# A Sobel stage: its contraction in three chunks of 128 rows in place of four of 96, the bias as a float32r product, and its loops written out

## The chip, the cores and the metric

The kernel runs on one core of one Trainium2 chip. The metric is the device time of one execution in microseconds (us). The kernel is one program of seven stages that follow one another; the change touches one of them, which takes some 290 us of the 3580.

## What is computed

Four image blocks follow one another on x (2 images, 192 channels, 112 by 112, f32): window attention with an MLP, a Sobel block, a ConvNeXt block, and a merged depthwise convolution. The Sobel block is the one that matters here:

```python
edge_x = _depthwise3x3(x, sobel_x, c)
edge_y = _depthwise3x3(x, sobel_y, c)
edges = jnp.concatenate([edge_x, edge_y], axis=1)          # 384 channels
fused = jnp.einsum('bchw,oc->bohw', edges, fusion_w) + fusion_b[None, :, None, None]
mu = jnp.mean(fused, axis=1, keepdims=True)
var = jnp.mean(jnp.square(fused - mu), axis=1, keepdims=True)
normed = (fused - mu) * jax.lax.rsqrt(var + EPS)
normed = normed * ln_w[None, :, None, None] + ln_b[None, :, None, None]
return x + jax.nn.gelu(normed, approximate=False)
```

## The kernel before

The MLP stage ahead of this one has already made the horizontal halves of both Sobel filters and stored them in DRAM: `d["u"]` (differences, for edge_x) and `d["v"]` (smoothed, for edge_y). The function `sobel` works through 28 steps (`NS`, 14 strips of 8 lines in each of 2 images). A strip is 7 blocks (`BX`) of 128 pixels. In words, step t goes through the engines so:

- **SP** loads four tiles, u and v for each half k of the channels (`xu`, `xv`, 96 partitions each, one buffer for each). Each load waits until VectorE has used up the tile of the step before. It stores the finished strip of five steps before (`SLAG`) from `X` to `scratch_x2`.
- **DVE** (VectorE) makes the vertical halves in `edges(t, k)`: an add of two views of `xu` (L1119) and a subtraction of two views of `xv` (L1122) into `edge`, which has two buffers. So L1119 waits until PE is done with step t-2 (`fused`). Between `edges(t, 0)` and `edges(t, 1)` stand the end of step t-4, `X + f` (L1131), which waits for the gelu, and the scale and shift of the normalised step t-3 (L1136 by `ln_w`, then L1138 by `ln_b`, which waits for L1136).
- **PE** (TensorE) makes, for each of the 7 blocks, one product of 384 rows in four chunks of 96 (L1187). The bias is a 97th row in the first chunk: a row of ones in `edge`, the bias in `wf`. The columns of the weights and of the bias are centred beforehand, so the mean of the result is zero. Each f32 product is two instructions for PE, so a step has 56. PSUM holds two steps; PE waits until the step two before has been read (`normed`).
- **ACT** (ScalarE) takes in its body for step t, in this order: the gelu of step t-4 (L1160), two squares with a sum of step t-1 (L1152), the seven scaled copies of step t-2 out of PSUM (L1168, `normed`; they wait for the reciprocal deviation `rs` and for L1131 of step t-4, which frees the buffer of `f`), and the other five squares of step t-1.
- **POOL** (GpSimd) adds epsilon to the seven sums (L1092, reads one small tile) and raises them to the power -0.5 (L1096, reads two) for step t-2.

The loops of all five queues run over two steps at a time (`run_steps` with U = 2) behind a head of 6 steps written out; SP loops over one step at a time. Nothing else orders the work: each engine takes its instructions in the order in which they are written, and waits on semaphores.

Of the kernel before, what the change touches and what calls it, by code (L numbers as in the profile page):

```python
# [14 lines left out]
ALU = mybir.AluOpType  # L15
# [994 lines left out]
def sobel(nc, a, d, X, PS, stack):  # L1010

    s = Scope(nc, "sobel", stack)

    wf = s.sb("wf", [CH + 1, 2 * KC, C])
    mean = s.sb("mean", [CH + 1, 2 * KC])
# [10 lines left out]
    uloaded, vloaded = s.sems("uloaded", KC), s.sems("vloaded", KC)  # L1026
    q = {x: s.sem(x) for x in ("wloaded", "ready", "wsum", "wmean", "centred", "ex", "ey", "fused", "squared", "var_ok",
                               "rstd", "normed", "scaled", "affine", "gelu", "added", "stored")}
    U, HEAD, LAG = 2, 6, 4
    SLAG = 5  # L1030
    READY = 2

    def psF(t, j):
        return PS[:, 4 * t.buf(2) + j // 2, j % 2 * 256:j % 2 * 256 + C]

    def in_blocks(t, e):
        return view(edge[0:CH, t.buf(2), e, 0, 0:1], [[8, 8], [64, 2 * BX], [1, 8]])

    def per_block(i):
        return view(row[:, i, 0:1], [[0, BX], [1, C]])  # L1040
# [1 line left out]
    def rows8(ap):  # L1042
        return ap.rearrange("p r (b c) -> p r b c", c=8)

    with nc.Block() as block:
        @block.sync
        def _(sp):
            sp.dma_start(wf[0:CH, :, :], a["L1_conv_fusion_wT"].rearrange("(k p) n -> p k n", p=CH)).then_inc(q["wloaded"], 16)
            sp.dma_start(wf[CH:CH + 1, 0, :], a["L1_conv_fusion_b"].partition_broadcast(1)).then_inc(q["wloaded"], 16)
# [16 lines left out]
            for img in range(IMG):  # L1066
                for j in range(SLAG):
                    t = Step(0, img * BY + j, 1)
                    load(t, img, 8 * j)
                    if t.reached(SLAG):  # L1070
                        store(t.back(SLAG))
                with sp.Fori(SLAG, BY) as g:
                    load(Step(g, img * BY, 1), img, g * 8)
                    store(Step(g, img * BY - SLAG, 1))
            for j in range(NS - SLAG, NS):
                store(Step(0, j, 1))
            sp.wait_ge(q["stored"], 16 * NS)

        @block.gpsimd
        def _(pool):  # L1080
            nc.gpsimd.memset(edge[CH:CH + 1, :, 0, :, :], 1.0).then_inc(q["ready"], 1)
            pool.wait_ge(q["ready"], 1)
            nc.gpsimd.memset(mhalf[:, :], -0.5).then_inc(q["ready"], 1)
            pool.wait_ge(q["ready"], 2)
# [12 lines left out]
            run_steps(pool, NS, U, HEAD, LAG, body)  # L1097

        @block.vector
        def _(dve):  # L1100
            dve.wait_ge(q["wloaded"], 64)
            for e in range(2 * KC):
                rows = CH + 1 if e == 0 else CH
                nc.vector.reduce_sum(mean[0:rows, e:e + 1], wf[0:rows, e, :], AX.X).then_inc(q["wsum"], 1)
            dve.wait_ge(q["wsum"], 2 * KC)
            for e in range(2 * KC):
                rows = CH + 1 if e == 0 else CH
                nc.vector.tensor_scalar(mean[0:rows, e:e + 1], mean[0:rows, e:e + 1], 1.0 / C, None, ALU.mult).then_inc(q["wmean"], 1)
            dve.wait_ge(q["wmean"], 2 * KC)
            for e in range(2 * KC):  # L1110
                rows = CH + 1 if e == 0 else CH
                nc.vector.tensor_scalar(wf[0:rows, e, :], wf[0:rows, e, :], mean[0:rows, e:e + 1], None, ALU.subtract).then_inc(q["centred"], 1)

            def edges(t, k):
                dve.wait_ge(uloaded[k], t.n * 16 + 16)
                if t.reached(2):
                    dve.wait_ge(q["fused"], t.n * BX - BX)
                u = xu[:, k, :, :]
                nc.vector.tensor_tensor(in_blocks(t, k), rows8(u[:, 0:8, :]), rows8(u[:, 1:9, :]), ALU.add).then_inc(q["ex"], 1)  # L1119
                dve.wait_ge(vloaded[k], t.n * 16 + 16)  # L1120
                v = xv[:, k, :, :]
                nc.vector.tensor_tensor(in_blocks(t, KC + k), rows8(v[:, 2:10, :]), rows8(v[:, 0:8, :]), ALU.subtract).then_inc(q["ey"], 1)  # L1122

            def body(t):
                if t.inside(NS):
                    edges(t, 0)
                c = t.back(4)
                if c.inside(NS):
                    dve.wait_ge(q["gelu"], c.n + 1)
                    strip = X[:, bass.ds(c.n * BX, BX), :]  # L1130
                    nc.vector.tensor_tensor(strip, strip, f[:, c.buf(2), :, :], ALU.add).then_inc(q["added"], 1)  # L1131
                b = t.back(3)
                if b.inside(NS):
                    fb = f[:, b.buf(2), :, :]
                    dve.wait_ge(q["normed"], b.n * BX + BX)
                    nc.vector.tensor_tensor(fb, fb, per_block(0), ALU.mult).then_inc(q["scaled"], 1)  # L1136
                    dve.wait_ge(q["scaled"], b.n + 1)
                    nc.vector.tensor_tensor(fb, fb, per_block(1), ALU.add).then_inc(q["affine"], 1)  # L1138
                if t.inside(NS):
                    edges(t, 1)  # L1140
            run_steps(dve, NS, U, HEAD, LAG, body)

        @block.scalar
        def _(act):
# [10 lines left out]
            def body(t):  # L1155
# [15 lines left out]
            run_steps(act, NS, U, HEAD, LAG, body)  # L1171

        @block.tensor
        def _(pe):
            pe.wait_ge(q["wloaded"], 64)
            pe.wait_ge(q["ready"], READY)
            pe.wait_ge(q["centred"], 2 * KC)

            def body(t):
                pe.wait_ge(q["ex"], t.n * KC + KC)  # L1180
                pe.wait_ge(q["ey"], t.n * KC + KC)
                if t.reached(2):
                    pe.wait_ge(q["normed"], t.n * BX - BX)
                for j in range(BX):
                    for e in range(2 * KC):
                        rows = CH + 1 if e == 0 else CH
# [441 lines left out]
```

## Time and profile before

| what | value |
|---|---|
| time, median of 3 runs | 3580.73 us (3580.53 to 3581.01) |
| the profiled execution's own time | 3581.64 us |
| its span | 3579.5 us |
| sobel stage: first load to first load of the next stage | 1825.9 to 2120.2 us |
| PE in it: first to last product | 1839.6 to 2101 us |

The profiled execution is 0.9 us slower than the median, and 2.1 us of it lie outside the span. Columns of the timeline are start, duration, engine, line, operation, output and inputs with their shapes; in brackets is the idle time of the engine ahead of the row and what ended it. Spans of POOL are rough. PE's mean durations (326 ns) are latencies; the pace is read from the distance between starts.

### The profile page before, as it was taken

The numbers are of one execution on the slowest core, as the hardware profiler recorded it, in microseconds if no ns is written. First come the engines' busy times: TensorE is split into PE (matmuls) and PEld (weight loads), VectorE is DVE, ScalarE is ACT, GpSimd is POOL, SyncE is SP. The second block draws the span as 40 slices with busy tenths as digits, with TensorE's granted clock in tenths as the row PEclk, the third lists the DMA queues.
The fourth block names the chain that finished last, engine by engine and source line by source line (L and its number), as shares of the span: only waits on it lengthen the run. The fifth ranks groups of instructions, "written<-read, shape, count | busy, mean of one in ns | idle before, by whom it ended". The sixth has DMA issues, their size and how long they took to land. (4 is left out here: it accounts for less than half of the span.)

```text
span 3579.5 us, 95798 instructions
## 1 busy us (share of the span) xinstructions
PE 3423.4 (96%) x31958; PEld 3312.3 (93%) x31958; DVE 2389.3 (67%) x5936; ACT 1790.2 (50%) x5312; POOL 1080.1 (30%) x1951
## 2 busy tenths in 40 slices
PE   7999999999799999999969969989999899989999
PEld 6888888888699999999969969989999899989999
DVE  5777777777556666666659979979999311125554
ACT  4666666666444444444426657659999200002222
POOL 3233333333244444444425520014444223320000
PEclk9999999999899999999989989999999899999999
DMA  1455566610011111111158865537777788877775
GB/s 34 123 197 192 198 239 235 233 58 23 23 34 51 51 51 51 50 51 51 50 141 256 247 188 198 196 124 201 198 198 199 221 253 253 251 228 228 227 227 174
DMA packets 472671, 554.97 MB, mean 155 GB/s; under 512 B 78259, under 2 KB 331957, under 8 KB 472373
## 3 DMA queue, kind: packets, MB, share of 16 engines
q1 hardware_dynamic: 447028, 531.65, 49.3%
q10 hardware_dynamic: 25344, 19.27, 1.7%
q8 instruction: 196, 3.21, 0.4%
q14 instruction: 103, 0.84, 0.1%
HBM read 392.56 MB, written 271.52 MB: 186 GB/s over the span
## 5 line engine op out<-in xcount | busy, mean ns | idle before, releaser
L1325 PE MATMUL PS<-dw_grid,dw_mats 128*128 128x196 f32 (+1 forms) x3840 | 624.0, 326 | 37.0 <-DVE dw_mats L1266 37.0
L1325 PEld LDWEIGHTS PS<-dw_grid,dw_mats 128*128 128x128 f32 x3840 | 623.5, 191 | 37.5 <-DVE dw_grid L1262 37.5
L1297 ACT ACTIVATE dw_res<-PS,dw_brow 128x196 f32<-128x196 f32 x192 | 81.5, 424 | 699.3 <-PE PS L1325 699.3
L981 PE MATMUL PS<-mlp_w,mlp_hid 128*128 128x192 f32 x2352 | 414.0, 326 | 0.5 <-ACT mlp_hid L796 0.5
L1262 DVE COPY dw_grid<-X 32x392 f32 (+3 forms) x480 | 290.3, 605 | 171.8 <-PE PS L1325 148.7
L1560 PE MATMUL PS<-gain,down_hid 128*128 128x192 f32 x2352 | 385.4, 328 | 3.6 <-DMA down_hid<-scratch_hid 3.6
L1560 PEld LDWEIGHTS PS<-gain,down_hid 128*128 128x128 f32 x2352 | 385.1, 191 | 3.9 <-DMA down_hid<-scratch_hid 3.9
L981 PEld LDWEIGHTS PS<-mlp_w,mlp_hid 128*128 128x128 f32 x2352 | 378.3, 190 | 0.8 <-ACT mlp_hid L796 0.8
L796 ACT ACTIVATE mlp_hid<-PS,mlp_b 128x256 f32<-128x256 f32 x588 | 247.0, 471 | 110.8 <-PE PS L787 110.8
L1187 PE MATMUL PS<-sobel_wf,sobel_edge 96*128 96x192 f32 (+1 forms) x1568 | 261.0, 328 | 29.2 <-DVE sobel_edge L1122 28.9
L1187 PEld LDWEIGHTS PS<-sobel_wf,sobel_edge 96*128 96x128 f32 (+1 forms) x1568 | 257.3, 191 | 32.9 <-issue 32.8
L1548 DVE TENSOR_TENSOR X<-PS,down_x 128x192 f32 (+1 forms) x196 | 70.0, 357 | 319.2 <-PE PS L1560 317.6
L796 ACT ACTIVATE hid_hid<-PS,hid_b 128x256 f32<-128x256 f32 x588 | 237.0, 471 | 34.4 <-PE PS L787 34.4
L529 ACT ACTIVATE att_vbd<-PS 64x96 f32<-64x96 f32 x784 | 194.4, 248 | 109.4 <-PE PS L625 102.5
L854 POOL COPY X<-mlp_x 128x192 f32 (+1 forms) x196 | 113.5, 579 | 429.0 <-DVE mlp_x L926 427.8
L537 ACT ACTIVATE att_qk<-PS,att_qbias 128x256 f32<-128x256 f32 x392 | 164.7, 471 | 148.6 <-PE PS L652 148.6
L926 DVE TENSOR_TENSOR mlp_x<-PS,X 128x192 f32<-128x192 f32 x196 | 70.0, 357 | 212.8 <-PE PS L981 195.2
L408 POOL TENSOR_SCALAR att_xn<-att_x,att_mv,att_rs 128x192 f32<-128x192 f32 x196 | 198.5, 1022 | 20.1 <-POOL att_rs L401 20.1
L397 POOL TENSOR_SCALAR att_ve<-att_mv 128x2 f32<-128x2 f32 x98 | 22.6, 231 | 593.9 <-DVE att_mv L440 593.9
L1540 POOL TENSOR_TENSOR down_x<-down_x,cvec 128x192 f32<-128x192 f32 x196 | 115.7, 590 | 272.1 <-DMA down_x<-scratch_x 272.1
L473 DVE TENSOR_REDUCE att_mx<-PS 128x8 f32<-128x512 f32 x196 | 135.6, 692 | 71.3 <-PE PS L641 71.2
L787 PE MATMUL PS<-mlp_ha_hi,mlp_wa_hi 128*128 128x256 f32 x588 | 174.7, 297 | 0.0
(217 smaller groups left out, 9284.2 us busy)
## 6 DMA issues: line engine op xcount, KB each, us to landing
scratch_hid<-hid_hid SPq DMA_DIRECT2D x196, 384.0 KB, 3.7
down_hid<-scratch_hid SPq DMA_DIRECT2D x196, 384.0 KB, 4.0
scratch_wide<-scratch_taps SPq DMA_DIRECT2D x64, 960.0 KB, 5.3
dw_raw<-scratch_wide SPq DMA_DIRECT2D x96, 640.0 KB, 4.3
scratch_wide<-scratch_taps SPq DMA_DIRECT2D x64, 768.0 KB, 4.7
dw_raw<-scratch_wide SPq DMA_DIRECT2D x96, 512.0 KB, 3.3
sobel_xv<-scratch_v SPq DMA_DIRECT2D x56, 420.0 KB, 5.0
scratch_u<-mlp_u SPq DMA_DIRECT2D x56, 378.0 KB, 3.0
```

The lines of the kernel that those rows point to most:

```text
L408: nc.gpsimd.tensor_scalar(xn[:, i, :], x[:, t.buf(XR) - 1 + i, :], mv[:, t.buf(4) - 1 + i, 0:1], rs[:, i:i + 1], ALU.subtract, ALU.mult).t ...
L473: nc.vector.reduce_max(mx[:, b.buf(2), :].rearrange("p (h e) -> p h e", e=2), s4, AX.X).then_inc(q["max"], 1)
L529: last = nc.scalar.activation(vbd[64 * e:64 * e + 64, b.buf(4), w, :, e, 0:HD], src, ACT.Identity)
L537: nc.scalar.activation(qk[:, u.buf(2), ch, :], psQK[i], ACT.Identity, bias=qbias[:, ch:ch + 1]).then_inc(q["qk_ready"], 1)
L787: last = nc.tensor.matmul(self.psU[i][:, e * 256:(e + 1) * 256], w[:, m], h, start=(j == 0), stop=(j == len(terms) - 1))
L796: last = nc.scalar.activation(hid[:, m, :], self.psU[i][:, e * 256:(e + 1) * 256], ACT.Gelu, bias=self.b1[:, m:m + 1])
L981: last = nc.tensor.matmul(psD[i], hid[:, p.buf(2), m, i * 128:(i + 1) * 128], w2[:, m, :], start=(m == 0), stop=(m == MC - 1))
L1187: last = nc.tensor.matmul(psF(t, j), edge[0:rows, t.buf(2), e, j, :], wf[0:rows, e, :], start=(e == 0), stop=(e == 2 * KC - 1))
L1262: last = nc.vector.tensor_copy(dst, src)
L1325: last = nc.tensor.matmul(dst[:, :, ys, :], m, src, start=(i == 0), stop=(i == len(steps) - 1))
L1540: nc.gpsimd.tensor_tensor(x2[:, b.buf(R), :], x2[:, b.buf(R), :], cvec[:, :], ALU.add).then_inc(q["resid"], 1)
L1560: last = nc.tensor.matmul(PS[:, b.buf(R), 0:C], hid[:, b.buf(R), m, :], gain2[:, img, m, :], start=(m == 0), stop=(m == MC - 1))
```

## The change

The 384 rows of the contraction are cut at 128 and 256 in place of 96, 192 and 288. The rows are 192 of u and 192 of v, so the middle chunk holds the last 64 of u and the first 64 of v, both in a tile `xm` of 128 partitions. There are still four edge operations for VectorE in a step (`OPS`): u on 128 partitions, u on 64, v on 64, v on 128, all with the 896 elements in a partition that there were before. In a body for step t the two of u now stand ahead of the work for t-4 and t-3, and the two of v behind it. `xu` and `xm` have two buffers each, `xv` one.

The 97th row has no room in a full chunk. The bias becomes a fourth product for each block, `ones_r` by `bias_r`, over 33 rows in float32r: row 0 holds the bias rounded to float32r, row 32 what the rounding left, and the rows between are zero. VectorE makes these rows ahead of the first step, which takes three more operations (L1112, L1122, L1125). The two DMAs that bring the bias wait for GpSimd's clearing of the tile and are issued behind the four loads of step 0. All loops of the stage are written out (`unrolled`).

```diff
-    wf = s.sb("wf", [CH + 1, 2 * KC, C])
+    wf = s.sb("wf", [128, KT, C])
+    bias_r = s.sb("bias_r", [PARTS, C], F32R)
+    ones_r = s.sb("ones_r", [PARTS, 128], F32R)
-    xu = s.sb("xu", [CH, KC, 9, HW])
-    xv = s.sb("xv", [CH, KC, 10, HW])
-    edge = s.sb("edge", [CH + 1, 2, 2 * KC, BX, 128])
+    xu = s.sb("xu", [128, 2, 9, HW])
+    xm = s.sb("xm", [128, 2, 10, HW])
+    xv = s.sb("xv", [128, 1, 10, HW])
+    edge = s.sb("edge", [128, 2, KT, BX, 128])
...
+            def load(t):
...
+                parts = ((xu, slice(0, 128), 9, u[0:128]), (xm, slice(0, REST), 9, u[128:C]),
+                         (xm, slice(REST, 128), 10, v[0:REST]), (xv, slice(0, 128), 10, v[REST:C]))
+                for i, (ring, rows, lines, src) in enumerate(parts):
+                    n = ring.shape[1]
+                    if t.reached(n):
+                        sp.wait_ge(q["edges"], (t.n - n) * OPS + i + 1)
+                    sp.dma_start(ring[rows, t.buf(n), 0:lines, :], src).then_inc(loaded[i][t.buf(n)], 16)
...
+            load(Step(0, 0, NS))
+            sp.wait_ge(q["ready"], 1)
+            for at_ in (0, PARTS - 1):
+                sp.dma_start(bias[at_:at_ + 1, :], a["L1_conv_fusion_b"].partition_broadcast(1)).then_inc(q["wloaded"], 16)
...
             def body(t):
                 if t.inside(NS):
-                    edges(t, 0)
+                    across(t, 0, 0, slice(0, 128), xu)
+                    across(t, 1, 1, slice(0, REST), xm)
...
                 if t.inside(NS):
-                    edges(t, 1)
-            run_steps(dve, NS, U, HEAD, LAG, body)
+                    along(t, 2, 1, slice(REST, 128), xm)
+                    along(t, 3, 2, slice(0, 128), xv)
+            unrolled(NS, 4, body)
...
                 for j in range(BX):
-                    for e in range(2 * KC):
-                        rows = CH + 1 if e == 0 else CH
-                        last = nc.tensor.matmul(psF(t, j), edge[0:rows, t.buf(2), e, j, :], wf[0:rows, e, :], start=(e == 0), stop=(e == 2 * KC - 1))
+                    nc.tensor.matmul(psF(t, j), ones_r[:, :], bias_r[:, :], start=True, stop=False)
+                    for k in range(KT):
+                        last = nc.tensor.matmul(psF(t, j), edge[:, t.buf(2), k, j, :], wf[:, k, :], start=False, stop=(k == KT - 1))
                     last.then_inc(q["fused"], 1)
-            run_steps(pe, NS, U, HEAD, 0, body)
+            unrolled(NS, 0, body)
```

On VectorE, one step of the loop before, from its first edge operation on; REGISTER_ALU and ISA rows are address and semaphore work of the loop:

```order
L1119 TENSOR_TENSOR sobel_edge<-sobel_xu 96x8x14x8
L1122 TENSOR_TENSOR sobel_edge<-sobel_xv 96x8x14x8
L1129 REGISTER_ALU
L1131 ISA
L1131 TENSOR_TENSOR X<-X,sobel_f 128x1344
L1135 ISA
L1136 TENSOR_TENSOR sobel_f<-sobel_f,sobel_row 128x1344
L1137 REGISTER_ALU
L1138 TENSOR_TENSOR sobel_f<-sobel_f,sobel_row 128x1344
```

One step of the change at the same place (steady state):

```order
L1133 TENSOR_TENSOR sobel_edge<-sobel_xu 128x8x14x8
L1133 TENSOR_TENSOR sobel_edge<-sobel_xm 64x8x14x8
L1149 TENSOR_TENSOR X<-X,sobel_f 128x1344
L1154 TENSOR_TENSOR sobel_f<-sobel_f,sobel_row 128x1344
L1156 TENSOR_TENSOR sobel_f<-sobel_f,sobel_row 128x1344
L1139 TENSOR_TENSOR sobel_edge<-sobel_xm 64x8x14x8
L1139 TENSOR_TENSOR sobel_edge<-sobel_xv 128x8x14x8
```

There are still seven operations in a step and the same three in the middle; two u operations stand ahead of them in place of a u and a v, and the rows of the loop's own work are gone.

On SP's queue at the start of the stage, before:

```order
L1048 DMA sobel_wf<-in_L_conv_fusion_wT 96x4x192
L1049 DMA sobel_wf<-in_L_conv_fusion_b 1x192
L1051 DMA sobel_row<-in_L_conv_ln_w 128x192
L1051 DMA sobel_row<-in_L_conv_ln_b 128x192
L1057 DMA sobel_xu<-scratch_u 96x1008
L1060 DMA sobel_xv<-scratch_v 96x1120
L1057 DMA sobel_xu<-scratch_u 96x1008
L1060 DMA sobel_xv<-scratch_v 96x1120
```

and now:

```order
L1054 DMA sobel_wf<-in_L_conv_fusion_wT 128x3x192
L1056 DMA sobel_row<-in_L_conv_ln_w 128x192
L1056 DMA sobel_row<-in_L_conv_ln_b 128x192
L1067 DMA sobel_xu<-scratch_u 128x1008
L1067 DMA sobel_xm<-scratch_u 64x1008
L1067 DMA sobel_xm<-scratch_v 64x1120
L1067 DMA sobel_xv<-scratch_v 128x1120
L1076 DMA sobel_bias<-in_L_conv_fusion_b 1x192 x2
L1067 DMA sobel_xu<-scratch_u 128x1008
L1067 DMA sobel_xm<-scratch_u 64x1008
```

The bias was second; it is now two transfers behind the loads of step 0, and the loads of step 1 follow without a wait but for `xv`.

On PE, the loop before:

```order
L99 UNCONDITIONAL_BRANCH
L99 ISA
L1183 ISA
L1187 MATMUL PS<-sobel_wf,sobel_edge 128x192 x28
L1180 ISA
L1183 ISA
L1187 MATMUL PS<-sobel_wf,sobel_edge 128x192 x28
```

and the first blocks of the change, written out:

```order
L1201 MATMUL PS<-sobel_bias_r,sobel_ones_r 128x192
L1203 MATMUL PS<-sobel_wf,sobel_edge 128x192 x3
L1201 MATMUL PS<-sobel_bias_r,sobel_ones_r 128x192
L1203 MATMUL PS<-sobel_wf,sobel_edge 128x192 x3
L1201 MATMUL PS<-sobel_bias_r,sobel_ones_r 128x192
```

A block was four products of one kind; it is now one float32r product and three f32 products.

## Rows read from the trace of the kernel before

**Rows 1.** Stretch 1900 to 1950: busy us (instructions) of PE, PEld, DVE, ACT, POOL; clock, DMA share, GB/s.

```profile
1900.00:1950.00 50.00, 49.91 (x303) 49.04 (x302) 47.17 (x39) 30.28 (x115) 27.05 (x11) 1.00 0.87 258
```

**Rows 2.** Waits, 1860 to 2100: engine, line, releaser: total us, times, longest.

```profile
ACT sobel_f L1168 <- POOL sobel_rs L1096: 54.2, 24, 3.2
...
DVE sobel_edge L1119 <- PE PS L1187: 18.7, 24, 5.4
...
PEld PS L1187 <- issue: 3.7, 12, 0.4
```

**Rows 3.** Timeline of ACT, 1851 and 1860: start us, us; the waits in brackets.

```profile
1851.25 0.33 ACT L1152 ACTIVATE sobel_sq<-PS 128x192 bf16<-128x192 f32 x1 [0.57 <-PE PS L1187]
...
1860.37 0.33 ACT L1152 ACTIVATE sobel_sq<-PS 128x192 bf16<-128x192 f32 x1 [0.57 <-PE PS L1187]
```

**Rows 4.** Timeline of DVE, 1906 to 1926, two steps and a piece.

```profile
1906.33 1.09 DVE L1119 TENSOR_TENSOR sobel_edge<-sobel_xu 96x896 f32<-96x896 f32 x1 [0.24 <-PE PS L1187]
...
1907.34 1.08 DVE L1122 TENSOR_TENSOR sobel_edge<-sobel_xv 96x896 f32<-96x896 f32 x1
...
1908.34 1.55 DVE L1131 TENSOR_TENSOR X<-X,sobel_f 128x1344 f32 x1
...
1911.40 1.56 DVE L1138 TENSOR_TENSOR sobel_f<-sobel_f,sobel_row 128x1344 f32<-128x1344 f32 x1
...
1913.87 1.08 DVE L1122 TENSOR_TENSOR sobel_edge<-sobel_xv 96x896 f32<-96x896 f32 x1
...
1917.97 1.56 DVE L1131 TENSOR_TENSOR X<-X,sobel_f 128x1344 f32 x1
...
1926.88 1.55 DVE L1131 TENSOR_TENSOR X<-X,sobel_f 128x1344 f32 x1
```

**Rows 5.** Timeline of POOL, 1906 to 1921.

```profile
1906.99 0.54 POOL L1092 TENSOR_SCALAR sobel_ve<-sobel_ss 128x7 f32<-128x7 f32 x1 [4.60 <-ACT sobel_sq L1152]
...
1907.70 5.03 POOL L1096 TENSOR_TENSOR sobel_rs<-sobel_ve,sobel_mhalf 128x7 f32<-128x7 f32 x1 [0.16 <-POOL sobel_ve L1092]
...
1918.11 2.79 POOL L1096 TENSOR_TENSOR sobel_rs<-sobel_ve,sobel_mhalf 128x7 f32<-128x7 f32 x1 [0.16 <-POOL sobel_ve L1092]
```

**Rows 6.** Timeline of ACT, 1912 to 1918.

```profile
1912.77 2.29 ACT L1168 ACTIVATE sobel_f<-PS,sobel_rs 128x192 f32<-128x192 f32 x7 [2.65 <-POOL sobel_rs L1096]
...
1916.42 1.41 ACT L1160 ACTIVATE sobel_f<-sobel_f 128x1344 f32<-128x1344 f32 x1
```

**Rows 7.** Timeline of PE at 700 (float32r terms) and at 1507 (plain f32).

```profile
700.66 0.34 PE L625 MATMUL PS<-att_wa_hi,att_ha_hi 128*128 128x192 f32 x1
700.83 0.28 PE L625 MATMUL PS<-att_wa_lo,att_ha_hi 128*128 128x192 f32 x1
700.94 0.27 PE L625 MATMUL PS<-att_wa_hi,att_ha_lo 128*128 128x192 f32 x1
...
1507.17 2.11 PE L981 MATMUL PS<-mlp_w,mlp_hid 128*128 128x192 f32 x12
...
1509.12 0.60 PE L758 MATMUL PS<-mlp_ident,mlp_xn 128*128 128x128 f32 x4
```

**Rows 8.** Timeline of all engines at the start of the sobel stage.

```profile
1827.11 0.41 SPq L1051 DMA_DIRECT2D sobel_row<-in_L_conv_ln_b  x1
...
1832.92 1.13 DVE L1104 TENSOR_REDUCE sobel_mean<-sobel_wf 97x1 f32<-97x192 f32 x4 [10.72 <-DMA sobel_row<-in_L_conv_ln_b]
...
1835.37 1.08 DVE L1119 TENSOR_TENSOR sobel_edge<-sobel_xu 96x896 f32<-96x896 f32 x1
...
1839.60 2.90 PE L1187 MATMUL PS<-sobel_wf,sobel_edge 97*128 97x192 f32 x8 [28.85 <-DVE sobel_edge L1122]
```

**Rows 9.** Stretch 1835 to 1837, columns as in rows 1.

```profile
1835.00:1837.00 2.00, 0.00 (x0) 0.00 (x0) 2.00 (x4) 0.00 (x0) 0.00 (x0) 0.50 0.65 160
```

**Rows 10.** Timeline of POOL, then of DVE, at 1852.

```profile
1852.61 2.18 POOL L1096 TENSOR_TENSOR sobel_rs<-sobel_ve,sobel_mhalf 128x7 f32<-128x7 f32 x1
...
1853.33 1.08 DVE L1119 TENSOR_TENSOR sobel_edge<-sobel_xu 96x896 f32<-96x896 f32 x1
```

More of the change, by code:

```diff
@@ L1025, in sobel, with in_blocks @@
     mhalf = s.sb("mhalf", [128, BX])
-    uloaded, vloaded = s.sems("uloaded", KC), s.sems("vloaded", KC)
-    q = {x: s.sem(x) for x in ("wloaded", "ready", "wsum", "wmean", "centred", "ex", "ey", "fused", "squared", "var_ok",
+    loaded = [s.sems("loaded%d_" % i, 2) for i in range(4)]
+    q = {x: s.sem(x) for x in ("wloaded", "ready", "wsum", "wmean", "centred", "edges", "fused", "squared", "var_ok",
                                "rstd", "normed", "scaled", "affine", "gelu", "added", "stored")}
-    U, HEAD, LAG = 2, 6, 4
     SLAG = 5
-    READY = 2
+    READY = 3
+    OPS = 4
     def psF(t, j):
         return PS[:, 4 * t.buf(2) + j // 2, j % 2 * 256:j % 2 * 256 + C]
-    def in_blocks(t, e):
-        return view(edge[0:CH, t.buf(2), e, 0, 0:1], [[8, 8], [64, 2 * BX], [1, 8]])
+    def in_blocks(t, e, rows):
+        return view(edge[rows, t.buf(2), e, 0, 0:1], [[8, 8], [64, 2 * BX], [1, 8]])
     def per_block(i):
@@ L1064, in store @@
                 sp.dma_start(d["x2"][bass.ds(t.n * BX, BX)].rearrange("b p c -> p b c"), X[:, bass.ds(t.n * BX, BX), :]).then_inc(q["stored"], 16)
[L1066 to L1074, printed above, removed]
+            load(Step(0, 0, NS))
+            sp.wait_ge(q["ready"], 1)
+            for at_ in (0, PARTS - 1):
+                sp.dma_start(bias[at_:at_ + 1, :], a["L1_conv_fusion_b"].partition_broadcast(1)).then_inc(q["wloaded"], 16)
+            for j in range(1, NS):
+                load(Step(0, j, NS))
+                if j >= SLAG:
+                    store(Step(0, j - SLAG, NS))
             for j in range(NS - SLAG, NS):
-                store(Step(0, j, 1))
+                store(Step(0, j, NS))
             sp.wait_ge(q["stored"], 16 * NS)
@@ L1080, in _ @@
         def _(pool):
-            nc.gpsimd.memset(edge[CH:CH + 1, :, 0, :, :], 1.0).then_inc(q["ready"], 1)
+            nc.gpsimd.memset(bias[:, :], 0.0).then_inc(q["ready"], 1)
             pool.wait_ge(q["ready"], 1)
+            nc.gpsimd.memset(ones[:, :], 1.0).then_inc(q["ready"], 1)
             nc.gpsimd.memset(mhalf[:, :], -0.5).then_inc(q["ready"], 1)
-            pool.wait_ge(q["ready"], 2)
+            pool.wait_ge(q["ready"], READY)
             def body(t):
@@ L1106, in _ @@
[L1106 to L1115, printed above, removed]
+            rows = [wf[:, k, :] for k in range(KT)] + [bias[:, :]]
@@ new lines, in _ @@
+            means = [mean[:, k:k + 1] for k in range(KT)] + [mean[0:PARTS, KT:KT + 1]]
+            dve.wait_ge(q["wloaded"], 16 * 5)
+            dve.wait_ge(q["ready"], READY)
+            nc.vector.tensor_copy(ones_r[:, :], ones[:, :])
+            for r, m in zip(rows, means):
+                nc.vector.reduce_sum(m, r, AX.X).then_inc(q["wsum"], 1)
+            dve.wait_ge(q["wsum"], KT + 1)
+            for m in means:
+                nc.vector.tensor_scalar(m, m, 1.0 / C, None, ALU.mult).then_inc(q["wmean"], 1)
@@ new lines, in _ @@
+            dve.wait_ge(q["wmean"], KT + 1)
+            for r, m in zip(rows, means):
+                nc.vector.tensor_scalar(r, r, m, None, ALU.subtract).then_inc(q["centred"], 1)
+            dve.wait_ge(q["centred"], KT + 1)
+            nc.vector.tensor_copy(bias_r[:, :], bias[:, :]).then_inc(q["centred"], 1)
+            dve.wait_ge(q["centred"], KT + 2)
+            low = slice(PARTS - 1, PARTS)
+            nc.vector.tensor_tensor(bias_r[low, :], bias[low, :], as_f32(bias_r[low, :]), ALU.subtract).then_inc(q["centred"], 1)
@@ L1121, in edges, with along @@
-                v = xv[:, k, :, :]
-                nc.vector.tensor_tensor(in_blocks(t, KC + k), rows8(v[:, 2:10, :]), rows8(v[:, 0:8, :]), ALU.subtract).then_inc(q["ey"], 1)
+                nc.vector.tensor_tensor(in_blocks(t, k, rows), rows8(src[:, 0:8, :]), rows8(src[:, 1:9, :]), ALU.add).then_inc(q["edges"], 1)
+            def along(t, i, k, rows, src):
+                n = src.shape[1]
+                src = src[rows, t.buf(n), :, :]
+                dve.wait_ge(loaded[i][t.buf(n)], t.turn(n) * 16 + 16)
+                nc.vector.tensor_tensor(in_blocks(t, k, rows), rows8(src[:, 2:10, :]), rows8(src[:, 0:8, :]), ALU.subtract).then_inc(q["edges"], 1)
@@ L1139, in body @@
                 if t.inside(NS):
[L1140 to L1141 removed]
+                    along(t, 2, 1, slice(REST, 128), xm)
+                    along(t, 3, 2, slice(0, 128), xv)
+            unrolled(NS, 4, body)
         @block.scalar
```

40 lines of the change are left out of this document (14 added, 26 removed).

## The prediction

> **What bounds the kernel now.** The stages follow one another, so I read only the stretch of this stage, by windows first. Between 1900 and 1950 us PE is busy for 49.91 of 50 us at the full clock, DVE for 47.17, ACT for 30.28, and the DMA engines for 0.87 of the time [rows 1]. So PE sets the pace, but DVE is 5% behind it, and that decides this case. The waits agree: PE waits for nobody; its weight loads meet 12 short gaps of issue, 3.7 us in all; DVE waits for PE (18.7 us in 24 times), ACT for POOL's L1096 (54.2 us) [rows 2].
>
> The pace, part by part. In the steps written out ahead of the loop the last block of a step reaches ACT at 1851.25 and of the next at 1860.37, with ACT waiting for PE both times: 9.12 us for a step [rows 3], which is 56 products of 0.163 us. In the loop two steps take 18.54 us (L1131 at 1908.34 and at 1926.88) [rows 4], or 9.27 for one; the 0.30 above twice 9.12 are what one turn of the loop costs PE.
>
> DVE's own step, read from start to start where it has no idle time: L1119 at 1906.33, L1131 at 1908.34, L1138 at 1911.40, the last L1122 at 1913.87, and 1.01 more for it (the distance of the first two rows): 8.55 us [rows 4].
>
> Then a round through four engines. L1131 starts at 1908.34. POOL has begun L1096 at 1907.70, but it takes 5.03 us and ends at 1912.73, that is 1.33 behind the start of L1138 at 1911.40 [rows 4, 5]. L1138 waits for L1136, so there DVE is free for an instant. ACT's L1168 starts at 1912.77 and takes 2.29, then come five squares, the gelu at 1916.42 for 1.41, and the next L1131 at 1917.97 [rows 4, 6]. From L1131 to L1131 that is 9.63 us without any wait for PE. In the next step L1096 begins at 1918.11, just behind the start of L1131 that had waited for the gelu, and takes 2.79 [rows 5]; that round is short. I call these the long and the short step; they alternate over the whole loop. The long one gets its length from POOL being held off by DVE.
>
> **The change part by part.**
>
> PE. Removed: 2 of 8 f32 instructions in each block, so 6 stay. Plain f32 products of 192 columns go at 1.95 us for 12 (L981 at 1507.17 to L758 at 1509.12), 0.1625 each [rows 7]. Added: a float32r product of 192 columns. The same width stands in the attention: 0.17 us from the first of a run to the second, 0.11 from the second to the third [rows 7]. In the change every one stands between f32 products, so I take the 0.17; bounds 0.11 and, if it went like f32, 0.33. A block becomes 6 x 0.1625 + 0.17 = 1.145, a step 8.0 us against 9.12 (bounds 7.6 and 9.1). PE alone would give 28 x (9.27 - 8.0) = 35 us.
>
> DVE. Four edge operations of 896 elements in a partition stay four, whatever the partitions; I cost them unchanged, and the step at 8.55. So from the step on in which all seven operations are there, DVE covers most of PE's gain.
>
> Where the stall goes. With PE at 8.0 it no longer fills the time; the long step of 9.63 is made of DVE, POOL and ACT alone and is untouched by the change. What follows depends on how often it comes:
> - It alternates as now: 9.63 and then 8.55 (DVE without idle), 9.09 for a step.
> - It never comes: 8.55.
> - I take one long in three: (9.63 + 8.55 + 8.55) / 3 = 8.91. PE starts its product when L1168 has freed PSUM, 6.7 us behind the long step's L1131 (1915.06 against 1908.34 [rows 4, 6]), and ends it 8.0 later, which is 5.1 behind the next L1131. So the sums reach POOL while the last edge operation of DVE's step runs, and L1096 falls between the two u operations. The one L1096 that began with only edge operations around it began at 1852.61 and took 2.18, so it got in at the next boundary, 1853.33 [rows 10]. A step later PE's end falls some 1 us later against DVE, L1096 begins right ahead of L1131 as at 1907.70, and is held for long again.
>
> Sum for the steps: the first three steps have no L1131 yet, and behind the last product comes a tail that no edge operation holds up, so four steps gain PE's full 9.12 - 8.0 = 1.12, 4.5 us. The other 24 gain 9.27 - 8.91 = 0.36, 8.6 us. The loop's 0.30 a turn is inside that.
>
> The start of the stage costs. Today ln_b, issued at 1827.11, lands at 1832.92; DVE takes 2.45 us for the centring and 4.2 for the edges, and PE starts at 1839.60 [rows 8]. In the change the last thing that DVE waits for is the bias, behind four loads of 1.6 MB in the same queue. The DMA engines are still at 0.65 between 1835 and 1837 [rows 9], where step 0's loads end, so I take 1837 for its landing: 4 us later. The three added small operations, each with a semaphore, take some 1 us (a group of four reductions took 1.13 in the same place [rows 8]). Together 5 us; bounds 1 (the small transfers slip past) and 8 (they land with a wait of their own). What is queued behind that wait is all of DVE, and PE behind it; nothing hides it.
>
> Nothing for the rest: POOL's clearing of one row is replaced by two short ones, 10 us ahead of their use; ACT has 20 of 50 us idle [rows 1]. The second buffers I cost at nothing: DVE does not wait for a load among its waits now. But the loads stand in SP's order behind `xv`, which is single and waits for the end of DVE's step, so u and the middle of the next step have one DVE step, as now. DMA work is 0.87 x 9.27 = 8.1 us a step [rows 1], under 8.55, so the cover holds at 8.91 with 0.8 to spare and at 8.55 with 0.5.
>
> Sum: 5.0 - 4.5 - 8.6 = -8.1 us, -0.23%. The profiled execution stands 0.9 above the median; taken from the median, 3580.7 - 8.1 = 3572.6 us.
>
> **The rivals.**
>
> - The round alternates as now, 9.09: for it speaks that it does so eleven times in the loop. 5.0 - 4.5 - 24 x 0.18 = -3.8: 3576.9 us.
> - POOL is never held for long, DVE fills its time, 8.55: -16.8 or, with the setup's lower bound, -20: 3563.9 us. For it speaks the short step, in which L1096 waits for one operation only [rows 5]. Against it the long step: begun at 1907.70, L1096 lets the ends of two operations pass and gets in at the third [rows 4, 5]. The Trainium skill, SBUF — State Buffer, section "A bandwidth-pool intuition that's wrong", has the blocked engine go on some 115 ns behind the end of the DVE operation; by that the long step would not exist, L1096 would end within 3 us of L1131, and the time would be this rival's. The trace disagrees in the long step.
> - Slower: the held time grows. If DVE has no idle time and also L1092 must wait for the instant ahead of L1138, L1096 begins 3.3 us behind L1131 and gets in only at the end of DVE's step at 6.6; 1.4 for itself, 2.3 for L1168 and 2.9 for squares and gelu make 13.2 in place of 9.63. Each such step costs 3.6 us; two cancel the forecast's gain, four or five make it slower than now by 0.2%, one in three gives 29 - 8 = +21: 3602 us. For it speaks that in the change DVE is nearly full; against it that L1092 now gets in at once (0.54 us at 1906.99, while an edge operation runs) [rows 5].
> - The float32r product costs as much as an f32 one: PE stays at 9.1, only the loop's 0.15 a step is won, and the setup costs: 5 - 4 = +1: 3582 us. The rows of the attention speak against it.
>
> **How the numbers follow.** A measurement tells 0.2%, 7.2 us, from no change. Chances: one long step in three or near it 0.36, half of it beyond 7.2; alternating 0.27, nearly all within; DVE filled 0.24; POOL starved 0.09; float32r dear or the start worse 0.04. That gives faster 0.47, same 0.43, slower 0.10. The range reaches from DVE filled with a cheap start (3561) to alternating with a dear start (3581). The forecast's own, with its start between 1 and 8 us, is 3568.6 to 3575.6.
>
> **What the profile of the change would show.** PE with idle time of 0.5 to 1 us ahead of each step, ended by the last edge operation or by ACT's copies out of PSUM, and a step's products over in 8.0 us. A mean distance of the additions to X of 8.9; rows of the -0.5 power of 5 us in one step of three. PE's first product 5 us later behind the stage's first load, with DVE waiting for the bias. DVE's share above 0.95. The forecast is wrong if the power's rows are all short (then 3564), all or half long (3577 or more), or if DVE waits for loads.

## The result, and the profile after

The changed kernel takes 3612.88 us (median of 4 runs, 3605.15 to 3613.77), the kernel before 3580.87 (3580.53 to 3581.72): a ratio of 1.0082, 95% interval 1.0067 to 1.0097. It is slower by 0.8%, where 0.2% faster was forecast, and outside the range.

The same stretch as [rows 1], of the changed kernel (busy us of PE, PEld, DVE, ACT, POOL; clock, DMA share, GB/s):

```profile
1900.00:1950.00 50.00, 50.00 (x243) 39.03 (x243) 43.18 (x35) 28.62 (x107) 29.00 (x10) 1.00 0.81 233
```

PE is still the busy one, at the full clock, with 243 instructions in place of 303. DVE has lost 4 us of work. So PE does fewer instructions and each takes longer. The weight loads (PEld) had filled 49.04 us; now 11 of 50 are free. The waits of the stretch of [rows 2] say where:

```profile
ACT sobel_f L1187 <- POOL sobel_rs L1103: 61.4, 22, 2.9
DVE sobel_edge L1133 <- PE PS L1203: 44.1, 24, 7.8
...
PEld PS L1201 <- issue: 37.3, 166, 0.2
```

DVE waits for PE in every step, and the engine's weight-load side stands idle 166 times ahead of the bias product's weights, with nothing named as the releaser ("issue"). One and a half blocks on PE, weight loads first, then matmuls:

```profile
1911.06 0.18 PEld L1201 LDWEIGHTS PS<-sobel_bias_r,sobel_ones_r 33*128 33x128 f32 x1 [0.23 <-issue]
1911.34 0.95 PEld L1203 LDWEIGHTS PS<-sobel_wf,sobel_edge 128*128 128x128 f32 x6
1912.51 0.18 PEld L1201 LDWEIGHTS PS<-sobel_bias_r,sobel_ones_r 33*128 33x128 f32 x1 [0.22 <-issue]
...
1911.06 0.35 PE L1201 MATMUL PS<-sobel_bias_r,sobel_ones_r 33*128 33x192 f32 x1
1911.34 1.24 PE L1203 MATMUL PS<-sobel_wf,sobel_edge 128*128 128x192 f32 x6
1912.51 0.35 PE L1201 MATMUL PS<-sobel_bias_r,sobel_ones_r 33*128 33x192 f32 x1
```

From one L1201 to the next is 1.45 us: 0.28 to the first f32 product, and 1.17 for six instructions that at 0.1625 each should take 0.975. The weight load of L1201 begins when its matmul begins, not ahead of it, and that of the next L1203 too. Neither switch, into the bias product or out of it, has its weights ready. A step of seven such blocks takes 10.17 us, against 9.27 before:

```profile
1901.06 1.09 DVE L1133 TENSOR_TENSOR sobel_edge<-sobel_xu 128x896 f32<-128x896 f32 x1 [1.32 <-PE PS L1203]
...
1907.71 1.09 DVE L1139 TENSOR_TENSOR sobel_edge<-sobel_xm 64x896 f32<-64x896 f32 x1
1908.83 1.09 DVE L1139 TENSOR_TENSOR sobel_edge<-sobel_xv 128x896 f32<-128x896 f32 x1
1911.24 1.09 DVE L1133 TENSOR_TENSOR sobel_edge<-sobel_xu 128x896 f32<-128x896 f32 x1 [1.32 <-PE PS L1203]
```

The start, to be held against [rows 8]: the stage's first transfer, DVE's first instruction, PE's first product.

```profile
1828.87 0.42 SPq L1054 DMA_DIRECT2D sobel_wf<-in_L_conv_fusion_wT  x1
...
1839.88 0.22 DVE L1112 CAST sobel_ones_r<-sobel_ones 33x128 fp32r<-33x128 f32 x1 [14.76 <-DMA sobel_bias<-in_L_conv_fusion_b]
...
1847.70 0.50 PE L1201 MATMUL PS<-sobel_bias_r,sobel_ones_r 33*128 33x192 f32 x1 [34.04 <-DVE sobel_edge L1139]
```

PE starts 18.8 us behind the stage's first transfer (before: 13.7, from 1825.93 to 1839.60), so +5.2. The account: 28 x (10.17 - 9.27) = 25.2 and 5.2 give 30.4; from the stage's first transfer to that of the next stage it is 325.3 us against 294.3, +31.0. The spans differ by 32.5, the rest lying outside the stage. The stage itself starts 3 us later, but stage starts differ by that much between kernels that are alike up to there (1825.2 to 1831.9 in the runs below), so I compare lengths of the stage.

### The profile page after: what moved, and what is told of

It is laid out like the page before. It is cut to its first block and busy times, and to the rows that moved or that the text cites. A ratio compares the mean times of both kernels' runs of the same rounds, so it can differ in the third digit from the quotient of the medians.

```text
span 3612.0 us, 94747 instructions
## 1 busy us (share of the span) xinstructions
PE 3449.7 (96%) x31762; PEld 3278.8 (91%) x31762; DVE 2392.7 (66%) x5939; ACT 1787.8 (49%) x5312; POOL 1101.8 (31%) x1952
## 5 line engine op out<-in xcount | busy, mean ns | idle before, releaser
L796 ACT ACTIVATE hid_hid<-PS,hid_b 128x256 f32<-128x256 f32 x588 | 236.6, 470 | 34.3 <-PE PS L787 34.3
L1203 PE MATMUL PS<-sobel_wf,sobel_edge 128*128 128x192 f32 x1176 | 245.6, 346 | 0.0
L1203 PEld LDWEIGHTS PS<-sobel_wf,sobel_edge 128*128 128x128 f32 x1176 | 187.4, 191 | 19.4 <-issue 0.3
```

What stands on the lines that cost most here:

```text
L796: last = nc.scalar.activation(hid[:, m, :], self.psU[i][:, e * 256:(e + 1) * 256], ACT.Gelu, bias=self.b1[:, m:m + 1])
L1203: last = nc.tensor.matmul(psF(t, j), edge[:, t.buf(2), k, j, :], wf[:, k, :], start=False, stop=(k == KT - 1))
```

## The experiments

The theory after the result was that the switch of type, float32 to float32r and back, stops the weights from being loaded ahead. The rival was the switch of contraction rows, 128 to 33 and back. Each run changes only the sobel function, and its ratio is taken against runs of the kernel before on the same chip (their medians lie between 3580.0 and 3582.2 us, and a single run beside the last gave 3584.1).

**Bias product in plain float32, 33 rows.** With the ones at 0.5, as both rows now hold the whole bias:

```
-  nc.tensor.matmul(psF(t, j), ones_r[:, :], bias_r[:, :], start=True, stop=False)
+  nc.tensor.matmul(psF(t, j), ones[:, :], bias[:, :], start=True, stop=False)
```

> The changed kernel with the bias product as plain float32 (two instructions over the same 33 rows, ones of 0.5 against the bias in both rows, so the sum is the same). Nothing else moves. In the changed kernel a block takes 1.453 us, of which six float32 instructions at the pace of before (0.1625 us) explain 0.975. Theory 'switch' (going from float32 to float32r and back costs, because no weights are loaded ahead across it): there is no switch left, eight instructions at 0.1625 make a block of 1.30 us, a step of 9.1 us where it now is 10.17, and a time of 3613 - 28 x 1.06 = 3583 us. Rival 'rows' (going from 128 contraction rows to 33 and back costs): the cost stays and one more instruction comes on top, a block of 1.6 us, a step of 11.3, 3645 us.

Measured: 3940.19 us, ratio 1.1002 (1.0984 to 1.1021). Both theories missed it. A block by PE's timeline, and then the stretch's row, with columns as in [rows 1]:

```profile
1901.77 1.00 PE L1201 MATMUL PS<-sobel_bias,sobel_ones 33*128 33x192 f32 x2
1902.71 2.29 PE L1203 MATMUL PS<-sobel_wf,sobel_edge 128*128 128x192 f32 x6
```

```profile
1900.00:1950.00 50.00, 50.00 (x128) 36.02 (x127) 17.53 (x14) 12.77 (x48) 11.60 (x4) 0.50 0.36 109
```

The granted clock is 0.50 (1.2 GHz) through the whole stage, though PE is never idle. A block takes 22.07 / 7 = 3.15 us; eight instructions at twice 0.1625 are 2.60, so 0.55 remain for switches, with no change of type left. The type theory is in trouble, as it allows for no such remainder; the clock is a second effect of its own, and the last two runs take it up.

**Bias product over 128 rows, float32r.** `bias`, `bias_r`, `ones` and `ones_r` are 128 rows deep, with zeros between:

```
-    bias_r = s.sb("bias_r", [PARTS, C], F32R)
+    bias_r = s.sb("bias_r", [128, C], F32R)
```

> The changed kernel with the float32r bias product over all 128 rows (ones and bias_r are 128 rows deep, zeros in 31 and the last 95 rows of bias_r). The type still changes twice a block, the number of rows no longer does. Theory 'switch': nothing changes, block 1.45 us, step 10.17, 3613 us. Rival 'rows': the product costs what the attention rows gave for one in a run, 0.11 to 0.17 us, block 1.09 to 1.14, PE's step under 8.0, the step then set by the round of DVE, POOL and ACT at about 8.9, and 3613 - 28 x 1.27 = 3577 us.

Measured: 3578.69 us, ratio 0.9994 (0.9984 to 1.0003). PE's timeline, weight loads first:

```profile
1869.19 0.19 PEld L1201 LDWEIGHTS PS<-sobel_bias_r,sobel_ones_r 128*128 128x128 f32 x1
1869.35 0.95 PEld L1203 LDWEIGHTS PS<-sobel_wf,sobel_edge 128*128 128x128 f32 x6
...
1869.22 0.38 PE L1201 MATMUL PS<-sobel_bias_r,sobel_ones_r 128*128 128x192 f32 x1
1869.44 1.16 PE L1203 MATMUL PS<-sobel_wf,sobel_edge 128*128 128x192 f32 x6
1870.30 0.38 PE L1201 MATMUL PS<-sobel_bias_r,sobel_ones_r 128*128 128x192 f32 x1
```

The block is 1.086 us, six at 0.1625 and 0.11. The weights are loaded ahead of their matmul again (by 0.03 and 0.09 us, from start to start), across the same two changes of type. The type theory falls; rows it is, at 1.453 - 1.086 = 0.367 us for the two switches of a block. But the step is 9.30 us in the mean, not 8.9, so that the time came close to the 3577 of "rows" is partly luck: more below.

**The 33-row product twice in a row.** The bias is added twice, so the result of the kernel differs.

```
   nc.tensor.matmul(psF(t, j), ones_r[:, :], bias_r[:, :], start=True, stop=False)
+  nc.tensor.matmul(psF(t, j), ones_r[:, :], bias_r[:, :], start=False, stop=False)
```

> The changed kernel with the float32r bias product issued twice in each block, one right behind the other (the bias is added twice). Theory 'switch': the second product is already in its type and costs only its own pace, 0.11 us by the attention rows, so block 1.56 us, step 10.9, and 3613 + 28 x 0.77 = 3634 us. Rival 'each product is dear' (0.48 us for one of 33 rows, whatever stands ahead of it): block 1.93, step 13.5, 3706 us.

Measured: 3890.36 us, ratio 1.0865 (1.0847 to 1.0883), again at a granted clock of 0.50 throughout, so its time tells neither number. Its rows do:

```profile
1921.27 0.28 PEld L1201 LDWEIGHTS PS<-sobel_bias_r,sobel_ones_r 33*128 33x128 f32 x1 [0.44 <-issue]
1921.43 0.33 PEld L1202 LDWEIGHTS PS<-sobel_bias_r,sobel_ones_r 33*128 33x128 f32 x1
1921.94 1.78 PEld L1204 LDWEIGHTS PS<-sobel_wf,sobel_edge 128*128 128x128 f32 x6 [0.17 <-issue]
```

Of the two 33-row products only the second has its weights loaded ahead (from 1921.43, for a matmul at 1921.60). The idle time stands at the two switches (0.44 and 0.17 us), not at each product.

**65 rows, and 64.** These fix where the switch begins: `PARTS` 65 or 64 in place of 33.

> The changed kernel with the float32r bias product over 65 rows in place of 33 (zeros in all rows but 0 and 32). The run with 128 rows gave a block of 1.086 us, the changed kernel's 33 rows 1.453, and the kernel before went from 97 rows to 96 in every block at no cost to be seen (eight instructions at 0.1625 us). Theory 'row mode' (TensorE is drained when the number of contraction rows goes across 64, and not by other changes of it): 65 rows cost nothing extra, block 1.09 us, and the time is that of the 128-row run, 3579 us. Rival 'any narrower product' (a product that leaves the last quarter or half of the rows unused holds up the next): block stays between 1.2 and 1.45, 3590 to 3613 us.

> The same with 64 rows, one row less. Theory 'row mode': the drain is back in full, block 1.45 us, a step of 10.17, 3613 us. Rival (the cost depends on how many rows are unused): between the 65-row and the 33-row block.

Measured: 3579.49 us with 65 rows, ratio 0.9996 (0.9986 to 1.0005), and 3611.28 with 64 (one run). PE's timeline, of 65 and then of 64 rows:

```profile
1882.92 0.39 PE L1201 MATMUL PS<-sobel_bias_r,sobel_ones_r 65*128 65x192 f32 x1
1883.15 1.16 PE L1203 MATMUL PS<-sobel_wf,sobel_edge 128*128 128x192 f32 x6
```

```profile
1900.99 0.35 PE L1201 MATMUL PS<-sobel_bias_r,sobel_ones_r 64*128 64x192 f32 x1
1901.27 1.24 PE L1203 MATMUL PS<-sobel_wf,sobel_edge 128*128 128x192 f32 x6
1902.44 0.35 PE L1201 MATMUL PS<-sobel_bias_r,sobel_ones_r 64*128 64x192 f32 x1
```

One row makes the whole difference: 64 rows give the block of 33 rows (1.45, step 10.17), 65 rows that of 128 (step 9.30). The Trainium skill, TensorEngine Tiling (Array Packing), section "Tiling Modes", has row tilings of 32, 64 and 128 rows and says that changing the mode drains the engine (the work in it must end before the next begins); it gives no price, and does not say which mode an ordinary matmul takes. The traces fit it if matmuls of 64 rows or fewer run in another mode than those of 65 or more, which is my inference; what is measured is the price, 0.367 us for there and back. By the same inference the kernel before, with 97 rows and then 96, never changed modes, and its products did go at 0.163 us without a remainder.

**128 rows in plain float32.** The last corner of the table of type by rows.

> The version with the bias product over 128 rows, with that product in plain float32 (two instructions) in place of float32r. It fills the last corner of type by rows: float32r with 33 rows 1.453 us a block, float32r with 128 rows 1.086, float32 with 33 rows 3.15 (at a granted clock of 0.50). Theory 'row mode' (only going across 64 rows costs, the type costs nothing, and the low clock of the float32 run with 33 rows came with its drains): block 8 x 0.1625 = 1.30 us at a granted clock of 1.00, step 9.1, and since nearly every step of the kernel before took 9.1 to 9.4, 3579 to 3583 us. Rival 'float32 bias lowers the clock whatever its rows': granted clock 0.50, block 2.6, step 18.2, 3830 us.

Measured: 3588.26 us, ratio 1.0018 (1.0008 to 1.0027), clock 1.00 in the stage. PE's timeline:

```profile
1900.11 0.49 PE L1201 MATMUL PS<-sobel_bias,sobel_ones 128*128 128x192 f32 x2
1900.43 1.14 PE L1203 MATMUL PS<-sobel_wf,sobel_edge 128*128 128x192 f32 x6
1901.41 0.49 PE L1201 MATMUL PS<-sobel_bias,sobel_ones 128*128 128x192 f32 x2
```

The block is 1.30 as said. The time missed my numbers because I had left the later start (+5) out of them, and took the step at 9.1 to 9.3; its mean is 9.40. Four corners, block in us:

| bias product | 33 rows | 128 rows |
|---|---|---|
| float32r | 1.453 (3613 us) | 1.086 (3579 us) |
| float32 | 3.15 at clock 0.50 (3940 us) | 1.30 (3588 us) |

The corner at clock 0.50 can't be compared with the others; the last run below shows one block of it at the full clock, 1.67 us, which is 1.30 and 0.367 again.

**No bias product.** Its line is taken out, so the kernel leaves out the bias:

```
-                    nc.tensor.matmul(psF(t, j), ones_r[:, :], bias_r[:, :], start=True, stop=False)
```

> The changed kernel with the bias product left out altogether (fusion's bias is not added; the first float32 product of a block carries the start flag). It takes the disputed cost away and shows what the rest of the change makes of the step. PE's step should be 42 x 0.1625 = 6.8 us, so PE is idle and the round of DVE, POOL and ACT sets the period. By my forecast one step in three is long, 8.9 us, time 3613 - 28 x 1.26 = 3578 us; alternating as in the kernel before, 9.09, 3583; DVE filled, 8.55, 3568; every step long because the pow on POOL is held off in each, 9.6, 3598.

Measured: 3578.14 us, ratio 0.9999 (0.9989 to 1.0008). PE has an idle seventh of the stretch:

```profile
1900.00:1950.00 50.00, 42.76 (x243) 41.05 (x241) 47.18 (x38) 31.11 (x119) 20.45 (x10) 0.95 0.88 266
```

The time is the 3578 that I had said for one long step in three, but by luck: the step is 9.24 us in the mean, not 8.9. The sum had 28 x 1.26 = 35 us. The steps gave 23 x (10.17 - 9.24) = 21, and the rest of the stage's 34.3 us (291.0 against 325.3) came from the first steps, 6.8 and 7.3 us long, and from the last, which I had not counted apart. So with PE's product free of charge the kernel is still no faster than before: the second half of my forecast was off as well, by something that is not PE.

**The bias transfers first.** On the 128-row version, the wait for `ready` and the two transfers are moved ahead of `ln_w`:

```
             sp.dma_start(wf[:, :, :], a["L1_conv_fusion_wT"]...)
+            sp.wait_ge(q["ready"], 1)
+            for at_ in (0, PARTS - 1):
+                sp.dma_start(bias[at_:at_ + 1, :], ...)
             for i, name in enumerate(("ln_w", "ln_b")):
...
             load(Step(0, 0, NS))
-            sp.wait_ge(q["ready"], 1)
-            for at_ in (0, PARTS - 1):
-                sp.dma_start(bias[at_:at_ + 1, :], ...)
```

> The 128-row version with the two transfers of the bias issued ahead of ln_w, ln_b and the four loads of step 0, instead of behind them. In the 128-row run VectorE's first instruction of the stage waited for the bias until 1839.26, 11.6 us after the stage's first transfer was issued, where the kernel before needed 7.0 us. Theory 'late bias' (that landing sets the start of the stage): the start comes 3 to 4.5 us earlier, 3579 becomes 3575 us. Rival (the loads of step 0 or ln_w and ln_b, which land about as late, set it): under 1 us, 3578 us.

Measured: 3574.70 us, ratio 0.9982 (0.9973 to 0.9991). Its DVE starts 6.8 us behind the stage's first transfer (1831.86), where the 128-row run needed 11.6, as the theory of the late bias had it:

```profile
1838.62 0.23 DVE L1112 CAST sobel_ones_r<-sobel_ones 128x128 fp32r<-128x128 f32 x1 [10.53 <-DMA sobel_row<-in_L_conv_ln_b]
```

**The order of the loads.** A second buffer for `xv` was to come first. That version did not fit and gave no time: with it the tile `f` needs 10752 B in each partition where 8384 are left. So the order was changed instead. On top of the bias-first version, of each step the loads of xu and xm go ahead of the xv load of the step before:

```
-            for j in range(1, NS):
-                load(Step(0, j, NS))
+            for j in range(1, NS + 1):
+                if j < NS:
+                    load(Step(0, j, NS), (0, 1, 2))
+                if j >= 2:
+                    load(Step(0, j - 1, NS), (3,))
```

> The bias-first version with one more change, in SyncE's queue alone: of each step the three loads of xu and xm come ahead of the xv load of the step before, so that they no longer queue behind a transfer that waits for VectorE's last operation (a second xv, which would do the same, doesn't fit in SBUF). In the 128-row run six steps in the bias-first version began with VectorE waiting for xu (7.9 us in all), and VectorE's own step is 8.77 us against a mean of 9.40. Theory 'queue': the waits for xu go, and as such a wait also upsets the round of POOL, ScalarE and VectorE behind it, the mean step falls to 9.0 to 9.1, 6 to 10 us below the bias-first run (3575), so 3565 to 3569 us. Rival 'DMA rate' (the transfers take some 8.1 us of 16 engines per step whatever their order, and land late anyway): within 2 us of 3575. Rival 'round' (the waits for xu only follow from steps that ran ahead; without them VectorE waits for PE or ScalarE instead): within 2 us too, with the wait shown under another name.

Measured: 3569.11 us, ratio 0.9961 (0.9947 to 0.9974): the fastest version, and below both kernels. The interval just touches that of the bias-first run; the stage is 283.9 us long against its 291.2. SyncE's queue in the 128-row run, xv first and all else behind it:

```profile
1908.55 0.33 SPq L1067 DMA_DIRECT2D sobel_xv<-scratch_v  x1
1908.93 0.43 SPq L1071 DMA_DIRECT2D scratch_x<-X  x1
1909.41 0.56 SPq L1067 DMA_DIRECT2D sobel_xu<-scratch_u  x1
```

DVE's waits in the bias-first run, 1863 to 2100, and the same of this one:

```profile
DVE sobel_edge L1133 <- DMA sobel_xu<-scratch_u: 7.9, 6, 2.0
DVE sobel_edge L1133 <- PE PS L1203: 6.3, 5, 3.3
DVE X L1149 <- ACT sobel_f L1179: 2.6, 5, 0.9
```

```profile
DVE X L1153 <- ACT sobel_f L1183: 5.4, 3, 4.2
DVE sobel_edge L1137 <- PE PS L1207: 2.9, 2, 2.7
DVE sobel_edge L1143 <- DMA sobel_xv<-scratch_v: 2.8, 1, 2.8
```

The waits for xu are gone, and the waits left lie in the first steps. From the sixth step to the last, every one takes 8.77 or 8.78 us, which is DVE without idle time, and the -0.5 power stands in one and the same place:

```profile
1911.33 2.18 POOL L1107 TENSOR_TENSOR sobel_rs<-sobel_ve,sobel_mhalf 128x7 f32<-128x7 f32 x1
```

```profile
1900.00:1950.00 50.00, 44.58 (x279) 42.81 (x278) 49.45 (x42) 33.39 (x123) 15.10 (x12) 1.00 0.88 268
```

DMA's share is 0.88 (0.87 in the kernel before), so the DMA rate was not the limit; the order was. The reorder has a price at the head of the stage: the xv of step 1 now queues behind loads of step 2 and lands late, and VectorE waits for it:

```profile
1857.08 1.09 DVE L1143 TENSOR_TENSOR sobel_edge<-sobel_xv 128x896 f32<-128x896 f32 x1 [6.25 <-DMA sobel_xv<-scratch_v]
```

From VectorE's first xu operation to its sixth it takes 44.0 us, against 38.8 in the bias-first run; the steps behind give back 13. Keeping the old order for the first steps alone was not tried.

The profiled executions of the 128-row and the bias-first runs were the slowest of theirs, 3.9 and 8.2 us above their medians. So their waits may be larger than those of a usual execution.

**The kernel before, loops unrolled.** All five `run_steps` and the `Fori` of the loads written out, nothing else.

> The kernel before with its sobel loops unrolled and nothing else (four chunks of 96 rows). It prices one part of the change by itself: each turn of the loop cost PE 0.30 us in 2 steps. Expected by my account: 11 turns x 0.30 = 3 us faster, 3577 to 3578 us. Rival (straight code loads more instructions and costs as much as it saves): 3580 to 3583 us.

Measured: 3580.76 us, ratio 0.9995 (0.9986 to 1.0004). The time is the rival's (3580 to 3583) and can't be told from no change. In the one profiled execution the stage is 292.6 us long against 294.3, so unrolling gave at most 1.7 of the 3 us that I had counted. Whether loading the longer code took the rest was not looked at.

**What holds the clock down.** The float32 run with 33 rows again, with float32 products of zeros over 128 rows ahead of the first step, into a bank that the stage starts afresh:

```
+            pe.wait_ge(q["ready"], READY)
+            for i in range(40):
+                nc.tensor.matmul(PS[:, 7, 0:C], junk[:, 0:128], junk[:, :], start=True, stop=True)
             pe.wait_ge(q["centred"], KT + 3)
```

> The run with the float32 bias product over 33 rows (3940 us; its granted clock was 0.50 from the first product to the last), with 40 more float32 products of zeros over 128 rows ahead of the first step, while TensorE would wait for the inputs anyway; they write a bank that the stage starts afresh. So the clock should be at 1.00 when the first step begins. Theory 'it only never rose' (the low clock is where the stage happened to start and its stream can't lift it): the stage stays at 1.00, block 1.30 + 0.37 for the two drains = 1.67 us, step 11.7, and 3613 + 28 x 1.5 = 3655 us. Rival 'its stream doesn't hold the clock': the granted clock falls back to 0.50 a few us into the stage, and the time is again about 3930 to 3940 us.

Measured: 3941.56 us (one run), inconclusive: the 40 products ended at 1841.55, and the first step began at 1845.20 with the clock back at 0.50.

> The warm-up run with 54 products in place of 40. The 40 brought the granted clock to 1.00 from about 1831 on but ended 3.65 us before the first step, which began at 0.50 again; 14 more at 0.325 us each cover those 3.65 us and 0.9 more. Theory 'it only never rose': the first step begins at 1.00 and the stage stays there, block about 1.67 us, step 11.7, about 3655 us. Rival 'its stream doesn't hold the clock': the first blocks run at 1.67, then the granted clock goes to 0.50 and the block to 3.15, and the time is again about 3935 to 3940 us.

Measured: 3944.14 us (one run). PE's first blocks, and the windows around them:

```profile
1847.45 0.56 PE L1206 MATMUL PS<-sobel_bias,sobel_ones 33*128 33x192 f32 x2 [1.71 <-DVE sobel_edge L1141]
...
1849.12 0.59 PE L1206 MATMUL PS<-sobel_bias,sobel_ones 33*128 33x192 f32 x2
1849.64 2.07 PE L1208 MATMUL PS<-sobel_wf,sobel_edge 128*128 128x192 f32 x6
1851.64 1.01 PE L1206 MATMUL PS<-sobel_bias,sobel_ones 33*128 33x192 f32 x2
```

```profile
1847.40:1849.10 1.70, 1.65 (x8) 1.24 (x8) 1.70 (x2) 0.00 (x0) 0.00 (x0) 1.00 0.46 63
1849.10:1850.00 0.90, 0.90 (x5) 0.66 (x5) 0.87 (x2) 0.00 (x0) 0.00 (x0) 0.94 0.83 289
1850.00:1860.00 10.00, 10.00 (x27) 7.38 (x26) 1.52 (x2) 1.47 (x8) 0.00 (x0) 0.50 0.98 289
```

Here the first block takes 1.67 us at 1.00, which is 8 x 0.1625 and the 0.367 of the switches, with no change of type in it. Then the clock falls to 0.50 and stays. PE had a gap of 1.71 us ahead of the first step, so the fall at 1850 may owe something to that gap; that it never comes back in 600 us of unbroken work does not. This stream doesn't hold the full clock. The changed kernel's does, with the same two switches a block and one instruction less: it began at 0.50, and its third block, at 1852.91, already takes 1.46 us. What sets these two apart was not settled.

## Why the prediction was wrong

- **PE's block: the step that failed.** I priced the float32r product at 0.17 us, from the attention's rows, "bounds 0.11 and, if it went like f32, 0.33". Its own time is 0.11, the lower bound. What I left out is that it has 33 contraction rows and its neighbours 128: two switches, 0.367 us a block, so the product comes to 0.48 in all, outside my bounds. The rows that I took it from have 128 rows on both sides [rows 7]. So the block is 1.453 for 1.145 and PE's step 10.17 for 8.0, above the 9.12 of before, and everything that I built on PE falling behind DVE had no ground. The error between 3572.6 and 3612.9 is 40 us, and the 128-row run, which takes away the switches and nothing else that costs time, is 34 us faster. The rival "as dear as an f32 one" (3582) asked the right question with the wrong cause and 0.33 us in place of 0.48; I gave it, together with a worse start, a chance of 0.04.
- **DVE's step, 8.55.** It is 8.77. The xv operation starts 1.12 us behind that of xm's other half (1907.71, 1908.83), not 1.01, and the other 0.11 us lies between the addition of `ln_b` and the edge operation behind it. So what surrounds the four edge operations was not quite "unchanged"; why these two distances grew was not looked into.
- **The round, one long step in three.** Not seen in the changed kernel: PE sets its pace, the power takes 5.11 us in 24 of 28 steps and costs nothing. The 128-row run shows what I had meant to forecast, and there the second step failed: mean 9.30 for 8.91, so the stage is 295.6 us long against 294.3 before, where 8 us less was forecast. Of the 0.39 us, 0.22 are DVE's own step. The other 0.17 are waits beyond those that I had allowed, in an execution 0.14 us a step above the median. I had costed the one that starts them at nothing, though I named its cause: "the loads stand in SP's order behind `xv`". With the queue reordered all waits of DVE were gone from the sixth step on, at a DMA share of 0.88. So the long steps of this version hung on the late xu; they were no rhythm of DVE and POOL alone.
- **DVE filled, 3563.9.** As a rival for this change it is refuted. As a state it exists: the last version is in it, at 8.77. Its place in the round decides the power's time: begun 0.27 us behind xu's operation it takes 2.18 us; begun in the changed kernel 0.28 us behind xm's (1902.35) it takes 5.11, and so lets the ends of two operations of DVE pass.
- **The start, +5.0.** Right, size and mechanism: +5.2, of it 4.0 for the landing of the bias, 0.9 for the setup and 0.2 for the edges. Moving the two transfers gave 4.8 back in the trace and 4.0 between the medians.
- **The chances.** "Faster 0.47" doesn't follow from its parts: half of 0.36 and 0.24 are 0.42.
- **Unrolling, 0.30 us a turn.** Inside the sum; by itself it gave 1.7 us in the profiled stage instead of 3, and nothing that the times can tell.

## What to carry to other kernels

Before adding a narrow matmul among wide ones, look at the contraction rows of both, not only at type and columns: padding the narrow operand with zeros to 65 rows or more cost nothing to be seen and saved 34 us here. A price taken from rows of the same width and type holds only if their neighbours are alike too. And where a queue is in order, put the load that waits longest last: one issue of 0.33 us in the wrong place kept VectorE from its own pace. Look at the first steps too, where the same order cost 5 us. A time that comes out as forecast proves little by itself: two of these did while the step behind them was 0.3 to 0.4 us off.

## What the runs showed of the hardware

- Going between 128 contraction rows and 64 or 33, and back, cost 0.367 us at the full clock; between 128 and 65, or 97 and 96, nothing to be seen; between float32 and float32r nothing (block 1.086 us, of it 0.975 the six float32 instructions).
- A float32r product of 192 columns over 65 or 128 rows in such a stream took 0.11 us, a third of the 0.325 of a float32 one.
- TensorE without an idle moment stayed at 1.2 GHz for a whole stage (600 us), and once fell to it from 2.4 GHz while it worked, some 2 us behind a gap of 1.71. All four runs that stayed there had two 33-row instructions in a block; those with one of 33 or 64 rows rose to 2.4 GHz.
- The power of a 128x7 tile on GpSimd took 1.51 to 5.11 us, by where in VectorE's step it began.
